# Q and K stored in runs of eight units per channel in an attention kernel on one core

## The chip, the cores and the metric

The kernel runs on one core of a Trainium2 chip. The metric is the device time of one execution in microseconds (us).

## The reference

The input is x of shape (8, 512, 256). After a layer norm, x is projected to Q, K and V, each 1024 wide, in segments of 128 tokens. A segment's 128 x 1024 block is then read as 16 heads of 128 rows by 64 channels, without a transpose: head h takes the 8 tokens 8h to 8h+7, and each token gives 16 rows of 64. Per head and segment:

```python
scores  = q @ k.T * scale                       # masked above the diagonal
att_dot = softmax(scores) @ v
sq, sk  = elu(q) + 1, elu(k) + 1
att_mem = (sq @ M) / (sq @ Z.T)
M, Z    = M + sk.T @ v, Z + sk.sum(rows)        # carried to the next segment
att     = gate * att_mem + (1 - gate) * att_dot
out     = att.reshape(128, 1024) @ Wo
```

A layer norm and a residual follow. Then comes a second block: three cycles of a small net of four layers that scales a "twist" of the row, and again a layer norm and a residual.

## The kernel before

Two sequences are worked on together as a pair, so a step is one pair and one of its 4 segments: 16 steps (`NT`), of which the first 12 run in a loop with four steps in its body. A step has 32 units (`UNITS`), a unit being one head of one of the two sequences. The units are handled in 4 groups g of 8 (`GU`), and in a group as 4 pairs (`GP`), because two units of 64 channels fill the 128 rows of the matmul array.

The order of the work is written out by hand, one function `step` for each engine, with semaphores between them:

- `project(i)`, L1109, TensorE: 12 fp16 matmuls make one half (32 channels) of Q (i = 0, 1), K (i = 2, 3) or V (i = 4, 5) of the *next* step in `x_bank`, a PSUM tile of 2 x 512 columns. Only one such tile exists, so `project(i + 1)` waits until half i has been taken out.
- `take_x(i)`, L814, VectorE: one instruction that transposes 32 x 32 blocks takes half i out of `x_bank` and stores it in `q_pos`, `k_pos` or `v_pos`. These hold in each partition one row of all 32 units, unit after unit, so a channel's 32 values are 64 words apart (68 for V).
- `turn(g)`, L1126, TensorE: transposes the four pairs of group g of Q and of K into a bank of `t_bank`. Each reads 128 consecutive words (two units side by side) as the weights of a matmul against the identity. Function `take_q` on ScalarE (L548 to L555) and VectorE (L823 to L828) turns them into fp16 parts for `scores(g)` (L1138, L1143).
- `exp_k(g)` (ScalarE, L564, L567) and `elu_k(g)` (GpSimd, L402, L405) make `sk`, which is elu(k) + 1 and has the layout of `k_pos`. `remember(g)`, L1187, TensorE, reads 128 consecutive words of `sk` as weights against two units of V, and VectorE adds the result to the memory `M` (L863). It isn't run in the last segment of a pair, so 12 of the 16 steps have it.
- `maxima` (L835), `probs` (L574), `turn_probs` (L1154), `read_out` (L1167, L1172), `divide` (L842, L845) and `gated` (L418 to L422) are the softmax, its product with V, the read from memory, and the gate. `to_rows` (L911, two instructions of VectorE) brings the attention back to token rows; `turn_att` (L1199) and `project_out` (L1214) multiply it with Wo.

`t_bank` has two banks that all the turning jobs share in a fixed order (`STEP_JOBS`). In particular `remember(0)` has two jobs, and the second (U0b) needs the bank that the next row tile (job N) leaves when VectorE's `split` (L775) has run; VectorE's order puts `split` right behind `take_x(3)`:

```python
                    y_norm(bp, s)
                    if not last:
                        take_x(bp, s, 3)
                    if ahead:
                        split(t_job(bp, s, "N"), s % 2, bp * NSEG + (s + 3))
                    maxima(bp, s, 2)
                    remember(bp, s, 0, last)
```

Of the kernel before, what the change touches and what calls it, by code (L numbers as in the profile page):

```python
# [5 lines left out]
ALU = mybir.AluOpType  # L6
ACT = mybir.ActivationFunctionType
# [17 lines left out]
GROUPS = 4  # L25
GU = UNITS // GROUPS
GP = GU // 2
DV1 = DK + 1
VS = DK + 4
EPS = 1e-5  # L30
# [34 lines left out]
def infini_block_kernel(nc, x, Wq, Wk, Wv, Wo, betas, memory0, z0, cw1, cb1, cw2, cb2, cw3, cb3,  # L65
                        cw4, cb4, gw1, gb1, gw2, gb2, gw3, gb3, adaptive_range, out):
    ctx = ExitStack()
    with ctx:
# [97 lines left out]
        assert top[0] <= gate_off, (top[0], gate_off)  # L166
        top[0] = attn_top

        def xt_cols(t, cols=2 * P):

            return bass.ds((t + 1) * 2 * P, cols)
# [119 lines left out]
        with nc.Block() as block:  # L291

            @block.sync
            def _(sp):
# [7 lines left out]
                sp.dma_start(Wo_sb, Wo.rearrange("(j p) n -> p j n", p=P)).then_inc(c_in, 16)  # L302
                for par in range(2):
                    sp.dma_start(M0[64 * par:64 * par + 64, :, 0:DK],
                                  memory0[0].rearrange("(j r) d e -> r d j e", r=2)[par]).then_inc(c_in, 16)
                    sp.dma_start(M0[64 * par:64 * par + 64, :, DK:DV1],
                                  z0[0].rearrange("(j r) a d -> r d j a", r=2)[par]).then_inc(c_in, 16)
# [58 lines left out]
            def _(pool):  # L366
# [30 lines left out]
                def elu_k(bp, s, g):  # L397

                    n = 4 * s + g
                    dst = sk[:, g * GU * DK:(g + 1) * GU * DK]  # L400
                    pool.wait_ge(ek_done, bp * 16 + n + 1)
                    pool.tensor_tensor(dst, dst, k_pos[s % 2][:, g * GU * DK:(g + 1) * GU * DK],  # L402
                                       ALU.add).then_inc(sk_part, 1)
                    pool.wait_ge(sk_part, bp * 16 + n + 1)
                    pool.tensor_tensor(dst, dst, ek, ALU.add).then_inc(sk_done, 1)  # L405

                def gated(bp, s, g, half):

                    n = 8 * s + 2 * g + half
                    mem, dot = (AB[half][:, m, :, :] for m in (1, 0))  # L410
                    u = GU * g + 4 * half
                    gt = gate[:, (u % H) * DK:(u % H + 4) * DK].rearrange("p (u e) -> p u e", u=4)
                    if n == 0:
                        pool.wait_ge(g_in, 16)
                    if g == 0 and half == 0:
                        pool.wait_ge(nat_done, bp * 8 + 2 * (s + 1))
                    pool.wait_ge(pm_free, bp * 32 + n + 2)
                    pool.tensor_tensor(mem, mem, dot, ALU.subtract).then_inc(mix, 1)  # L418
                    pool.wait_ge(mix, bp * 64 + 2 * n + 1)
                    pool.tensor_tensor(mem, mem, gt, ALU.mult).then_inc(mix, 1)  # L420
                    pool.wait_ge(mix, bp * 64 + 2 * n + 2)
                    pool.tensor_tensor(att[:, u * DK:(u + 4) * DK].rearrange("p (u e) -> p u e", u=4),  # L422
                                       mem, dot, ALU.add).then_inc(att_done, 1)

                def y_dev(bp, s):
# [84 lines left out]
            def _(act):  # L510
# [46 lines left out]

                def exp_k(bp, s, g):
                    n = 4 * s + g
                    cols = slice(g * GU * DK, (g + 1) * GU * DK)  # L560
# [6 lines left out]
                    act.activation(ek, sk[:, cols], ACT.Exp, scale=-1.0).then_inc(ek_done, 1)  # L567

                def probs(bp, s, g):
                    G = 4 * s + g  # L570
# [175 lines left out]
            def _(dve):  # L746
# [55 lines left out]
                def take_x(bp, s, i, first=False):  # L802


                    n = 6 if not first else 0
                    par = 0 if first else (s + 1) % 2
                    dve.wait_ge(x_full, bp * 24 + 6 * s + n + i + 1)
                    if not first and i == 2:

                        dve.wait_ge(sk_done, bp * 16 + (4 * s + 1))  # L810
                    dst = (q_pos, k_pos, v_pos)[i // 2][par].rearrange("p (u e) -> p e u", u=UNITS)
                    d0 = 32 * (i % 2)
                    bank = first_banks[i] if first else x_bank
                    dve.transpose(dst[:, d0:d0 + 32, :],  # L814
                                  bank.rearrange("p w (d c) -> p d w c", c=C)).then_inc(x_free, 1)

                def take_q(bp, s, g):
# [257 lines left out]
            def _(pe):  # L1075
# [81 lines left out]
                def read_out(bp, s, g, half):  # L1157

                    n = 8 * s + 2 * g + half
                    v = v_pos[s % 2].rearrange("p (u e) -> p u e", u=UNITS)  # L1160
# [4 lines left out]
                    for u in range(4):  # L1165
                        j, par = 2 * half + u // 2, u % 2
                        pe.matmul(pm_bank[:, 0, u * DV1:(u + 1) * DV1], PT[:, par, j, :],  # L1167
                                  v[:, GU * g + 2 * j + par, 0:DV1], start=True, stop=True)
# [7 lines left out]
                def remember(bp, s, g):  # L1176

                    if s == NSEG - 1:
                        return
                    v = v_pos[s % 2].rearrange("p (u e) -> p u e", u=UNITS)  # L1180
                    pe.wait_ge(sk_done, bp * 16 + (4 * s + g + 2))
                    for a in range(2):
                        b, n = t_job(bp, s, f"U{g}{'ab'[a]}")
                        pe.wait_ge(t_free[b], n)
                        for i in range(2):
                            u = GU * g + 4 * a + 2 * i
# [253 lines left out]
```

## Time and profile before

| what | value |
|---|---|
| time, median of 3 runs | 1279.06 us (1278.69 to 1281.06) |
| the profiled execution's own time | 1277.61 us |
| its span | 1275.8 us |
| TensorE matmul busy | 1084.4 us (85%) |
| TensorE weight load busy | 755.4 us (59%) |
| VectorE busy | 855.4 us (67%) |
| ScalarE busy | 611.2 us (48%) |
| GpSimd busy | 584.1 us (46%) |
| mean granted TensorE clock | 0.941 of full speed |

The attention part takes about the first 1060 us, the second block the rest. A weight load runs beside an earlier matmul, so its busy time is a row of its own (PEld) and not added to that of the matmuls (PE). A matmul with fp32 operands stands in the trace as two weight loads and two matmuls; an fp32 transpose stands as one of each.

### The profile page before, as it was taken

To read this page: it belongs to the slowest core of one execution; us is meant where nothing else is said; L and a number is where in the kernel's file an instruction comes from. 1 tells how busy PE (TensorE), PEld (TensorE's weight loads), DVE (VectorE), ACT (ScalarE), POOL (GpSimd) and SP (SyncE) were. 2 spreads that over 40 slices of the span, in tenths; PEclk is the share of its full clock that TensorE was granted. 3 is DMA by queue.
4 is the path that set the end of the run, shared out by engine and by line. 5 is a ranking of instruction groups with operands and counts; after the bars stand their busy time and mean duration, and the time that the engine had idled before them with its cause. 6 is when DMAs were issued, how large, how long until landed. Compare 5 with 4: busy or idle time off the path is not lost.

```text
span 1275.8 us, 20673 instructions
## 1 busy us (share of the span) xinstructions
PE 1084.4 (85%) x7172; PEld 755.4 (59%) x7172; DVE 855.4 (67%) x1492; ACT 611.2 (48%) x1291; POOL 584.1 (46%) x715
## 2 busy tenths in 40 slices
PE   3798989897888899878889888989888888999971
PEld 1475767664767676646666666676767675433331
DVE  4868686866686868656877687768686752434365
ACT  4354444444353535434545454535353553566662
POOL 2145454554454545444545454545454552322266
PEclk9999998988999989989999999999999988999995
DMA  5000000000000000000000000000000010300014
GB/s 161 20 10 9 10 9 10 10 11 9 10 9 9 9 10 10 10 11 2 17 10 9 9 10 9 10 10 9 9 2 9 1 28 1 140 0 0 1 33 99
DMA packets 14842, 24.02 MB, mean 19 GB/s; under 512 B 5264, under 2 KB 7056, under 8 KB 14224
## 3 DMA queue, kind: packets, MB, share of 16 engines
q1 hardware_dynamic: 14736, 22.63, 5.8%
q8 instruction: 63, 1.03, 0.3%
q14 instruction: 43, 0.35, 0.1%
HBM read 13.97 MB, written 8.65 MB: 18 GB/s over the span
## 4 chain that ended last, share of the span: by engine, by line
PE 49%; DVE 29%; issue 11%; ACT 7%; POOL 2%; DMA 1%; SPq 0%; DVEq 0%; POOLq 0%; ACTq 0%
PE ps L1109 12%; PE ps L1214 9%; DVE arena L814 7%; PE ps L1327 6%; PE ps L1167 5%; DVE arena L911 3%; PE ps L1340 3%; ACT arena L574 3%; PE ps L1172 3%; PE ps L1154 3%; DVE arena L758 2%; DVE arena L845 2%; DVE arena L824 2%; PE ps L1199 2%; DVE arena L828 2%
## 5 line engine op out<-in xcount | busy, mean ns | idle before, releaser
L1109 PE MATMUL ps<-arena 128*128 128x512 f16 x1152 | 274.0, 390 | 6.0 <-DVE arena L790 4.2
L574 ACT ACTIVATE arena<-ps,arena 128x128 f32<-128x128 f32 x512 | 139.3, 384 | 223.3 <-DVE arena L835 223.1
L814 DVE STREAM_TRANSPOSE arena<-ps 128x1024 f32<-128x1024 f32 x96 | 190.2, 1983 | 43.8 <-PE ps L1109 43.8
L1109 PEld LDWEIGHTS ps<-arena 128*128 128x128 f16 x1152 | 113.8, 100 | 131.8 <-issue 18.7
L418 POOL TENSOR_TENSOR arena<-arena 128x256 f32<-128x256 f32 x128 | 93.0, 727 | 161.7 <-DVE arena L845 161.7
L1167 PEld LDWEIGHTS ps<-arena 128*128 128x128 f32 x1024 | 134.8, 200 | 25.6 <-issue 17.3
L1167 PE MATMUL ps<-arena 128*128 128x65 f32 x1024 | 137.5, 280 | 13.2 <-DVE arena L845 11.8
L402 POOL TENSOR_TENSOR arena<-arena 128x512 f32<-128x512 f32 x64 | 81.3, 1270 | 125.5 <-ACT arena L567 125.5
L1214 PE MATMUL ps<-arena 128*128 128x256 f32 x544 | 122.0, 382 | 0.3 <-ACT arena L586 0.3
L388 POOL TENSOR_TENSOR arena<-arena 128x2 f32<-128x2 f32 x50 | 9.8, 196 | 238.8 <-DVE arena L754 238.8
L1214 PEld LDWEIGHTS ps<-arena 128*128 128x128 f32 x544 | 102.0, 190 | 16.1 <-ACT arena L586 1.4
L750 DVE BATCH_NORM_STATS2 arena<-arena 128x6 f32<-128x256 f32 x100 | 36.7, 409 | 111.0 <-ACT arena L592 97.4
L1154 PE MATMUL ps<-arena 128*128 128x128 f32 x512 | 82.7, 299 | 30.6 <-ACT arena L574 30.2
L1187 PE MATMUL ps<-arena 128*128 128x130 f32 x384 | 66.9, 312 | 41.4 <-DVE arena L775 24.1
L420 POOL TENSOR_TENSOR arena<-arena 128x256 f32<-128x256 f32 x128 | 93.1, 727 | 10.0
L422 POOL TENSOR_TENSOR arena<-arena 128x256 f32<-128x256 f32 x128 | 93.0, 727 | 10.0
L845 DVE TENSOR_TENSOR arena<-ps,arena 128x512 f32<-128x512 f32 x128 | 88.5, 691 | 13.1 <-DVE arena L842 0.8
L580 ACT ACTIVATE arena<-ps 128x1024 f32<-128x1024 f32 x64 | 65.7, 1026 | 64.4 <-PE ps L1154 64.4
L758 DVE TENSOR_SCALAR arena<-arena 128x256 f32<-128x256 f32 x100 | 68.7, 727 | 36.7 <-POOL arena L390 36.7
L1154 PEld LDWEIGHTS ps<-arena 128*128 128x128 f32 x512 | 62.5, 152 | 48.9 <-ACT arena L574 48.1
L835 DVE TENSOR_REDUCE arena<-ps 128x4 f32<-128x512 f32 x128 | 81.7, 678 | 12.5 <-PE ps L1143 12.1
L1327 PE MATMUL ps<-arena 128*128 128x512 f32 (+1 forms) x192 | 89.3, 609 | 0.8 <-ACT arena L687 0.8
(109 smaller groups left out, 1873.5 us busy)
## 6 DMA issues: line engine op xcount, KB each, us to landing
x_rows<-arena SPq DMA_DIRECT2D x17, 256.0 KB, 2.0
arena<-in_L_attn_x_dram SPq DMA_DIRECT2D x64, 64.0 KB
arena<-x_rows SPq DMA_DIRECT2D x4, 1024.0 KB, 8.0
out_dram<-arena SPq DMA_DIRECT2D x32, 128.0 KB, 2.9
arena<-in_L_attn_Wq_dram SPq DMA_DIRECT2D x1, 1024.0 KB, 12.2
arena<-in_L_attn_Wk_dram SPq DMA_DIRECT2D x1, 1024.0 KB, 14.4
arena<-in_L_attn_Wv_dram SPq DMA_DIRECT2D x1, 1024.0 KB, 17.4
arena<-in_L_attn_Wo_dram SPq DMA_DIRECT2D x1, 1024.0 KB, 13.0
```

Of the source, the lines that this page charges most:

```text
L418: pool.tensor_tensor(mem, mem, dot, ALU.subtract).then_inc(mix, 1)
L420: pool.tensor_tensor(mem, mem, gt, ALU.mult).then_inc(mix, 1)
L422: pool.tensor_tensor(att[:, u * DK:(u + 4) * DK].rearrange("p (u e) -> p u e", u=4), mem, dot, ALU.add).then_inc(att_done, 1)
L574: last = act.activation(Pr[:, par, j, :], s_bank[:, par, j * P:(j + 1) * P], ACT.Exp, bias=negm[:, par, j:j + 1])
L758: last = dve.tensor_scalar(dst[:, w * D:(w + 1) * D], src[:, w * D:(w + 1) * D], mv[:, w, 0:1], rs[:, w:w + 1], ALU.subtract, ALU.mult)
L814: dve.transpose(dst[:, d0:d0 + 32, :], bank.rearrange("p w (d c) -> p d w c", c=C)).then_inc(x_free, 1)
L845: dve.tensor_tensor(AB[half], rd[:, :, :, 0:DK], rr.rearrange("p m (u a) -> p m u a", a=1).to_broadcast([P, 2, 4, DK]), ALU.mult).then_inc ...
L1109: last = pe.matmul(bank[:, w, :], xc[:, lx, k, w * P:(w + 1) * P], W16[lw][:, k, i, :], start=(n == 0), stop=(n == 5))
L1154: last = pe.transpose(s_bank[:, par, j * P:(j + 1) * P], Pr[:, par, j, :], identf)
L1167: pe.matmul(pm_bank[:, 0, u * DV1:(u + 1) * DV1], PT[:, par, j, :], v[:, GU * g + 2 * j + par, 0:DV1], start=True, stop=True)
L1214: last = pe.matmul(t_bank[b][:, w * D:(w + 1) * D], attT[:, w, j, :], Wo_sb[:, j, :], start=(j == 0), stop=(j == 7))
L1327: done = pe.matmul(l1_bank[2 * j + c], w1[:, k, c * P:(c + 1) * P], XT[:, k, bass.ds((bb * 4 + (2 * j + 1)) * 2 * P, NB)], start=(k == 0), ...
```

## The change

A unit u is now written as u = 16 y + 8 r + h, with y the sequence of the pair, r = 0 or 1, and h = 0 to 7. `q_pos`, `k_pos` and `sk` are laid out as (y r, channel, h): for each channel, eight units (h) stand side by side. A pair is now made of units h and h + 8, no longer of two neighbours, and its 128 weights (r, channel) are read with a step of 8 words. `take_x` writes Q and K in runs of 8 words. V keeps its layout with a channel's units 68 words apart; its two units of a pair are now 8 units apart. The memory is loaded with the new pairing, the gate and the attention output are addressed accordingly, and `exp_k` and `elu_k` now work on runs of 4 words (the four pairs of a group). `ek` is written and read without gaps.

No instruction is added, removed or moved on any engine or queue, and none has another number of elements; what differs is how operands are addressed. The diff's core:

```diff
+HP = H // 2
+        def heads(a):
+            return a.rearrange("p (y z h) -> p y h z", y=2, h=HP)
+        def group(a, g):
+            return a.rearrange("p (y z h) -> p y z h", y=2, h=HP)[:, g // 2, :, GP * (g % 2):GP * (g % 2) + GP]
...
-                                  memory0[0].rearrange("(j r) d e -> r d j e", r=2)[par]).then_inc(c_in, 16)
+                                  memory0[0].rearrange("(r j) d e -> r d j e", r=2)[par]).then_inc(c_in, 16)
...
 # elu_k, GpSimd
-                    dst = sk[:, g * GU * DK:(g + 1) * GU * DK]
+                    dst, k = group(sk, g), group(k_pos[s % 2], g)
...
 # gated, GpSimd
-                    pool.tensor_tensor(att[:, u * DK:(u + 4) * DK].rearrange("p (u e) -> p u e", u=4),
+                    pool.tensor_tensor(att.rearrange("p (y r h e) -> p y h r e", y=2, r=2, h=HP)[:, g // 2, h:h + 2],
...
 # exp_k, ScalarE
-                    act.activation(sk[:, cols], k_pos[s % 2][:, cols], ACT.Relu, scale=-1.0).then_inc(rk_done, 1)
+                    act.activation(part, group(k_pos[s % 2], g), ACT.Relu, scale=-1.0).then_inc(rk_done, 1)
...
 # take_x, VectorE
-                    dst = (q_pos, k_pos, v_pos)[i // 2][par].rearrange("p (u e) -> p e u", u=UNITS)
+                    dst = (q_pos, k_pos, v_pos)[i // 2][par].rearrange(
+                        "p (u e) -> p e u" if i >= 4 else "p (v e h) -> p e v h", **(
+                            dict(u=UNITS) if i >= 4 else dict(v=UNITS // HP, h=HP)))
...
 # turn, TensorE
-                            u = GU * g + 2 * j
                             last = pe.transpose(t_bank[b][:, j * P:(j + 1) * P],
-                                                src[par][:, u * DK:(u + 2) * DK], identf)
+                                                heads(src[par])[:, g // 2, GP * (g % 2) + j], identf)
...
 # remember, TensorE
                             last = pe.matmul(t_bank[b][:, i * 2 * DV1:(i + 1) * 2 * DV1],
-                                             sk[:, u * DK:(u + 2) * DK], v[:, u:u + 2, 0:DV1],
+                                             heads(sk)[:, g // 2, h], v[:, h, :, 0:DV1],
                                              start=True, stop=True)
```

## Rows read from the trace of the kernel before

**Rows 1.** The page: busy time of each engine, and the chain's shares by engine.

```profile
PE 1084.4 (85%) x7172; PEld 755.4 (59%) x7172; DVE 855.4 (67%) x1492; ACT 611.2 (48%) x1291; POOL 584.1 (46%) x715
...
PE 49%; DVE 29%; issue 11%; ACT 7%; POOL 2%; DMA 1%; SPq 0%; DVEq 0%; POOLq 0%; ACTq 0%
```

**Rows 2.** Timeline of PE, us 434 to 500: start, us, engine, line, count, [idle before].

```profile
440.56 1.04 PE L1126 MATMUL ps<-arena 128*128 128x128 f32 x8
...
447.04 0.59 PE L1138 MATMUL ps<-arena 128*128 128x512 bf16 x2 [1.52 <-DVE arena L824]
...
449.79 1.08 PE L1167 MATMUL ps<-arena 128*128 128x65 f32 x8 [0.35 <-DVE arena L845]
...
464.36 0.60 PE L1126 MATMUL ps<-arena 128*128 128x128 f32 x4
...
472.02 1.24 PE L1187 MATMUL ps<-arena 128*128 128x130 f32 x4 [2.19 <-DVE arena L775]
...
475.62 1.94 PE L1187 MATMUL ps<-arena 128*128 128x130 f32 x8
...
487.36 0.71 PE L1187 MATMUL ps<-arena 128*128 128x130 f32 x4 [1.13 <-DVE arena L893]
...
496.07 1.06 PE L1187 MATMUL ps<-arena 128*128 128x130 f32 x8
497.44 1.08 PE L1167 MATMUL ps<-arena 128*128 128x65 f32 x8 [0.31 <-DVE arena L845]
```

**Rows 3.** Timeline of DVE, the same stretch: takes 0, 1 and 3 and their neighbours.

```profile
438.82 1.98 DVE L814 STREAM_TRANSPOSE arena<-ps 128x1024 f32<-128x1024 f32 x1 [0.42 <-PE ps L1109]
440.83 4.37 DVE L911 STREAM_TRANSPOSE arena<-arena 128x1024 f32<-128x1024 f32 x2
...
446.87 1.93 DVE L814 STREAM_TRANSPOSE arena<-ps 128x1024 f32<-128x1024 f32 x1
...
453.99 1.98 DVE L814 STREAM_TRANSPOSE arena<-ps 128x1024 f32<-128x1024 f32 x1 [1.66 <-PE ps L1109]
...
469.53 1.91 DVE L814 STREAM_TRANSPOSE arena<-ps 128x1024 f32<-128x1024 f32 x1
471.31 0.66 DVE L775 TENSOR_TENSOR arena<-ps,arena 128x512 f16<-128x512 f32 x1
```

**Rows 4.** Groups by line and form: count, busy us, mean ns, idle before.

```profile
L814 DVE STREAM_TRANSPOSE arena<-ps 128x1024 f32<-128x1024 f32 x96 | 190.2, 1983 | 43.8 <-PE ps L1109 43.8
...
L911 DVE STREAM_TRANSPOSE arena<-arena 128x1024 f32<-128x1024 f32 x34 | 74.2, 2243 | 2.1 <-POOL arena L422 1.6
...
L835 DVE TENSOR_REDUCE arena<-ps 128x4 f32<-128x512 f32 x128 | 81.7, 678 | 12.5 <-PE ps L1143 12.1
...
L1015 DVE BATCH_NORM_STATS2 arena<-ps 128x6 f32<-128x256 f32 x32 | 12.0, 415 | 0.0
```

**Rows 5.** The same view: ScalarE on 1024 elements, without and with a stepped read.

```profile
L580 ACT ACTIVATE arena<-ps 128x1024 f32<-128x1024 f32 x64 | 65.7, 1026 | 64.4 <-PE ps L1154 64.4
...
L515 ACT ACTIVATE arena<-arena 128x1024 f16<-128x1024 f32 x6 | 11.3, 1946 | 5.0 <-DMA arena<-in_L_attn_Wq_dram 5.0
```

**Rows 6.** The same view: the weight loads that the change touches, and GpSimd's part of `sk`.

```profile
L1126 PEld LDWEIGHTS ps<-arena 128*128 128x128 f32 x512 | 62.3, 148 | 12.6 <-DVE arena L863 6.0 <-issue 4.1
L1187 PEld LDWEIGHTS ps<-arena 128*128 128x128 f32 x384 | 55.4, 212 | 48.5 <-DVE arena L775 26.2 <-DVE arena L893 17.6 <-issue 2.2
...
L402 POOL TENSOR_TENSOR arena<-arena 128x512 f32<-128x512 f32 x64 | 81.3, 1270 | 125.5 <-ACT arena L567 125.5
```

**Rows 7.** Timeline of PEld: one `turn` and one `remember` of eight loads.

```profile
431.82 0.97 PEld L1187 LDWEIGHTS ps<-arena 128*128 128x128 f32 x8
...
440.45 0.91 PEld L1126 LDWEIGHTS ps<-arena 128*128 128x128 f32 x8
```

**Rows 8.** Windows: length, busy PE, PEld, DVE, ACT, POOL, granted clock, DMA share.

```profile
472.00:479.00 7.00, 6.98 (x33) 6.98 (x34) 4.95 (x14) 2.18 (x8) 1.17 (x2) 0.51 0.10 36
...
607.00:614.00 7.00, 7.00 (x51) 5.24 (x50) 5.56 (x18) 5.77 (x14) 2.47 (x5) 1.00 0.01 3
```

More of the change, by code:

```diff
@@ L304, in _ @@
                     sp.dma_start(M0[64 * par:64 * par + 64, :, 0:DK],
-                                  memory0[0].rearrange("(j r) d e -> r d j e", r=2)[par]).then_inc(c_in, 16)
+                                  memory0[0].rearrange("(r j) d e -> r d j e", r=2)[par]).then_inc(c_in, 16)
                     sp.dma_start(M0[64 * par:64 * par + 64, :, DK:DV1],
-                                  z0[0].rearrange("(j r) a d -> r d j a", r=2)[par]).then_inc(c_in, 16)
+                                  z0[0].rearrange("(r j) a d -> r d j a", r=2)[par]).then_inc(c_in, 16)
                 for dst, src in blocks(xrow[2], x_rows, 0, 2):
@@ L399, in elu_k @@
                     n = 4 * s + g
-                    dst = sk[:, g * GU * DK:(g + 1) * GU * DK]
+                    dst, k = group(sk, g), group(k_pos[s % 2], g)
                     pool.wait_ge(ek_done, bp * 16 + n + 1)
-                    pool.tensor_tensor(dst, dst, k_pos[s % 2][:, g * GU * DK:(g + 1) * GU * DK],
-                                       ALU.add).then_inc(sk_part, 1)
+                    pool.tensor_tensor(dst, dst, k, ALU.add).then_inc(sk_part, 1)
                     pool.wait_ge(sk_part, bp * 16 + n + 1)
-                    pool.tensor_tensor(dst, dst, ek, ALU.add).then_inc(sk_done, 1)
+                    pool.tensor_tensor(dst, dst, ek.rearrange("p (z h) -> p z h", h=GP),
+                                       ALU.add).then_inc(sk_done, 1)
                 def gated(bp, s, g, half):
                     n = 8 * s + 2 * g + half
-                    mem, dot = (AB[half][:, m, :, :] for m in (1, 0))
-                    u = GU * g + 4 * half
-                    gt = gate[:, (u % H) * DK:(u % H + 4) * DK].rearrange("p (u e) -> p u e", u=4)
+                    mem, dot = (AB[half][:, m, :, :].rearrange("p (h r) e -> p h r e", r=2) for m in (1, 0))
+                    h = GP * (g % 2) + 2 * half
+                    gt = gate.rearrange("p (r h e) -> p h r e", r=2, h=HP)[:, h:h + 2]
                     if n == 0:
@@ L559, in exp_k @@
                     n = 4 * s + g
-                    cols = slice(g * GU * DK, (g + 1) * GU * DK)
+                    part = group(sk, g)
                     if g == 0:
@@ L563, in exp_k @@
                     memory_stands(act, bp, s, g)
-                    act.activation(sk[:, cols], k_pos[s % 2][:, cols], ACT.Relu, scale=-1.0).then_inc(rk_done, 1)
+                    act.activation(part, group(k_pos[s % 2], g), ACT.Relu, scale=-1.0).then_inc(rk_done, 1)
                     act.wait_ge(rk_done, bp * 16 + n + 1)
                     act.wait_ge(sk_done, bp * 16 + (n + 1))
-                    act.activation(ek, sk[:, cols], ACT.Exp, scale=-1.0).then_inc(ek_done, 1)
+                    act.activation(ek.rearrange("p (z h) -> p z h", h=GP), part, ACT.Exp, scale=-1.0).then_inc(ek_done, 1)
                 def probs(bp, s, g):
@@ L810, in take_x @@
                         dve.wait_ge(sk_done, bp * 16 + (4 * s + 1))
-                    dst = (q_pos, k_pos, v_pos)[i // 2][par].rearrange("p (u e) -> p e u", u=UNITS)
+                    dst = (q_pos, k_pos, v_pos)[i // 2][par].rearrange(
+                        "p (u e) -> p e u" if i >= 4 else "p (v e h) -> p e v h", **(
+                            dict(u=UNITS) if i >= 4 else dict(v=UNITS // HP, h=HP)))
                     d0 = 32 * (i % 2)
                     bank = first_banks[i] if first else x_bank
-                    dve.transpose(dst[:, d0:d0 + 32, :],
+                    dve.transpose(dst[:, d0:d0 + 32],
                                   bank.rearrange("p w (d c) -> p d w c", c=C)).then_inc(x_free, 1)
@@ L1159, in read_out @@
                     n = 8 * s + 2 * g + half
-                    v = v_pos[s % 2].rearrange("p (u e) -> p u e", u=UNITS)
+                    v = v_pos[s % 2].rearrange("p (y r h e) -> p y h r e", y=2, r=2, h=HP)[:, g // 2]
                     pe.wait_ge(p_done, bp * 16 + 4 * s + g + 2)
@@ L1167, in read_out @@
                         pe.matmul(pm_bank[:, 0, u * DV1:(u + 1) * DV1], PT[:, par, j, :],
-                                  v[:, GU * g + 2 * j + par, 0:DV1], start=True, stop=True)
+                                  v[:, GP * (g % 2) + j, par, 0:DV1], start=True, stop=True)
                     memory_stands(pe, bp, s, g)
@@ L1179, in remember @@
                         return
-                    v = v_pos[s % 2].rearrange("p (u e) -> p u e", u=UNITS)
+                    v = v_pos[s % 2].rearrange("p (y r h e) -> p y h r e", y=2, r=2, h=HP)[:, g // 2]
                     pe.wait_ge(sk_done, bp * 16 + (4 * s + g + 2))
@@ L1185, in remember @@
                         for i in range(2):
-                            u = GU * g + 4 * a + 2 * i
+                            h = GP * (g % 2) + 2 * a + i
                             last = pe.matmul(t_bank[b][:, i * 2 * DV1:(i + 1) * 2 * DV1],
-                                             sk[:, u * DK:(u + 2) * DK], v[:, u:u + 2, 0:DV1],
+                                             heads(sk)[:, g // 2, h], v[:, h, :, 0:DV1],
                                              start=True, stop=True)
```

## The prediction

> **What bounds the kernel now.** I read the page's engine line first, then the chain, then the timelines of one step, then the groups by form. The page has TensorE's matmuls busy 85% of the span, VectorE 67%, but the chain that ended last gives TensorE only 49% and VectorE 29% [rows 1]. So neither engine alone sets the end: work passes between them. The timeline of one step shows where. The step from 434.7 to 498.9 us lasts 64.1 us, and TensorE stands still in it at a few places, nearly all ended by VectorE: 1.52 us before `scores(1)`, 0.35 us before `read_out(0, 1)`, 2.19 us before the second job of `remember(0)`, 1.13 us before that of `remember(2)`, 0.31 us before `read_out(3, 1)` [rows 2]. Between these TensorE runs without a gap. A saving on VectorE counts where it shortens such a wait; a loss on TensorE counts where it isn't swallowed by one.
>
> **The takes of Q and K.** `take_x` needs 1.98 us for 1024 elements per partition [rows 4]. The same engine, reading PSUM without a step, needs 0.415 us for 256 elements and 0.678 us for 512 [rows 4], which is 1.03 ns per further element, so 1024 would cost 0.678 + 512 x 1.03 ns = 1.21 us. The transposes of `to_rows`, stepped on both sides, need 2.24 us [rows 4]: a second stepped side adds 0.26 us, so steps do cost a transpose time. I take 1.22 us for a take that writes runs of 8 words, a saving of 0.76 us. The bounds are 0 (if the transposing itself is the slow part) and 0.8 us. The Trainium skill, Vector Engine (DVE) Microarchitecture Reference, section Measured stream behaviour on trn2, says that a port runs at full rate when its words come in aligned runs of two or more, and gives 1.71 ns per element for a hopping destination; the trace's 1.98 us over 1024 elements is near that. Four of six takes per step change (64 of the 96), some 49 us of VectorE's time. V's don't.
>
> What this buys, in the step shown, if nothing else changed:
> - Take 0 starts at 438.82 and `to_rows` follows it without a gap [rows 3]. All of it, `take_q(1)` behind it and so `scores(1)` come 0.76 us earlier; TensorE's 1.52 us wait has room for it.
> - Take 1 (446.87) stands before `divide(0, 0)`, which ends the 0.35 us wait [rows 2, 3]. TensorE gains that too: 1.1 us in all.
> - Take 2 waits 1.66 us for TensorE [rows 3] and ends no wait of TensorE. It gives nothing.
> - Take 3 (469.53) is followed by `split` at 471.31, which ends the 2.19 us wait [rows 2, 3]: a further 0.76 us.
>
> That is 1.9 us per step, 30 us over 16 steps, and 3 us at the start, where the first takes stand alone.
>
> **The weight loads.** `turn` has 32 loads per step and `remember` 32 in the 12 steps that have it: 512 and 384 [rows 6]. They follow one another closely: eight in 0.91 us and eight in 0.97 us [rows 7], that is one per 0.11 to 0.12 us, or 0.9 ns for each of the 128 words. As the eight matmuls of the turn take 1.04 us [rows 2], the load is what paces them, and a slower load would lengthen TensorE's own work. The trace has no stepped weight load, so I bound it. Low end: no cost, if TensorE fetches ahead. High end: the worst rate of any stepped access in the trace, 2243 / 1024 = 2.19 ns per word [rows 4], that is 280 ns per load, 0.17 us more than now. Between lies the cleanest pair of rows: ScalarE does 1024 elements in 1.026 us without a step and in 1.946 us with a stepped read [rows 5], 0.90 ns more per word. VectorE's take and ScalarE's stepped copy come to almost the same 1.9 ns per element although the engines differ, which speaks for a limit on the memory's side that a weight load would meet as well. I take 128 x 0.90 = 0.115 us more per load, 0.11 in the sums.
>
> The Trainium skill speaks on both sides. Advanced Engine Details and Errata, section SBUF Cachelines, says that accesses that each hit another 16-byte line pay a penalty, and a step of 8 words is 32 bytes; that is against this change, and it goes with my price. TensorE: Matmul & The Clock Gate, section LDWEIGHTS (loading the stationary operand), gives a load's time by its columns alone, P / 1.2 ns; by it the step is free, which is the first rival. The Trainium skill's Vector Engine (DVE) Microarchitecture Reference, in the section named above, has 2.50 ns for a step of 24 words, worse than for long ones; by an estimate from that figure a load would cost 0.21 us more, which is beyond rival 2. No row here shows any of the three for TensorE.
>
> **What the slower loads cost on the path.** Again in the step shown, in order, with 0.11 us per load:
> - `turn(1)`: 8 loads, 0.9 us. TensorE had 1.52 us of waiting behind it, of which 0.76 us is now gone; it just fits. TensorE stays 1.1 us ahead.
> - `turn(2)`, Q and K: 8 loads, 0.9 us. TensorE is then 0.3 us ahead. But the wait for `split` hangs on VectorE, which followed `project_out` and is some 0.75 us ahead, and with take 3 1.5 us. The first job of `remember(0)` is slower too, in that same wait. The wait shrinks from 2.19 to about 1 us and ends 1.5 us earlier.
> - the second job of `remember(0)`, `remember(1)`, `turn(3)`: 20 loads, 2.2 us without a wait to hide in, so TensorE is 0.8 us behind. VectorE, which left this row of work after `remember(1)`, is even. So the wait for L893 (1.13 us) swallows the 0.8 and nearly all of the 0.45 us of `remember(2)`'s first job.
> - its second job: 0.45 us, swallowed by the wait for ScalarE's exponentials. `turn(0)`: 0.9 us, and `remember(3)`: 0.9 us, less the 0.31 us wait [rows 2]: 1.4 to 1.5 us behind at the step's end.
>
> Sum with `remember`: +1.4 us. In the four steps without it only the turns count and the saving outweighs them: about -0.5 us.
>
> **The clock.** Behind the 2.19 us wait the granted clock is at 0.51 in one step, that is the lower of its two levels (1.2 GHz), and at 1.00 in another [rows 8]; eight matmuls of `remember` take 1.94 us at the lower and 1.06 us at the full level [rows 2]. About half of the steps fall there. With the wait cut to half I expect fewer falls, worth 0.4 us per step; the bounds are 0 and 0.9.
>
> **The rest.** ScalarE's and GpSimd's operands in runs of 4 words: I cost them at nothing. GpSimd waits 125.5 us in total before L402 [rows 6] and is 46% busy, ScalarE 48% [rows 1]. Were each of the 128 instructions of `elu_k` (1.27 us) to double, that would be 10 us per step on an engine with 34 us of rest, and only the residual add, queued behind `elu_k(2)`, would come late, by 2.5 us, with more than that before VectorE's statistics need it. The loads of the initial memory move the same bytes: nothing. `read_out` and `remember` read V in the same runs of 65 words: nothing.
>
> **Sum.** 12 x (1.4 - 0.4) + 4 x (-0.5 - 0.4) - 3 = 5.4 us. The swallowing above is exact to a few tenths per step, and take 1 and the falls of the clock may not give all that I credit; I round up to +10 us. The profiled execution took 1277.6 us, 1.5 us below the median of the runs: 1288 us, and the median with it within that 1.5 us. Its own range: -10 to +25 us, 1268 to 1303.
>
> **The rivals.**
> 1. *The step is free for weight loads.* For it: TensorE's reads may be buffered, and nothing in the trace shows the opposite. Against: two engines pay alike. Then the 1.9 us per step stay whole and the clock adds 0.4: 16 x 2.3 + 3 = 40 us less, **1238 us** (1225 to 1250).
> 2. *The loads become the bound.* At 0.17 us more per load `turn(1)` uses its whole wait, `turn(2)` eats the lead at `split`, and the wait for L893 no longer swallows `turn(3)` and `remember(1)`. The point from which it decides is some 0.12 us per load: up to there the waits hold most of it, beyond it nearly every load counts. Worked through in the same way, a step with `remember` ends 4.6 us behind and one without 2 us: 55 + 8, less 6 for the clock, **1335 us** (1305 to 1355).
> 3. *The takes get no shorter*, as the transposing is the slow part. Against it: `to_rows` reacts to a second stepped side. With the loads at +0.11 us, a step loses the 1.9 us too and ends about 3 us behind: **1330 us**.
>
> **How the numbers follow.** Forecast 0.34, rival 1 0.34, rival 2 0.25, rival 3 0.07. The forecast is the middle case and keeps a small edge, as the rows give its price directly. A measurement of this kernel can tell about 0.2%, 2.6 us. Rival 1 is faster throughout; of the forecast's 0.34, 0.08 lies below -2.6 us, 0.06 within, 0.20 above; rivals 2 and 3 are slower. Faster 0.42, same 0.06, slower 0.52. The range must reach into rivals 1 and 2: 1232 to 1348 leaves out about 0.2.
>
> **What would show it.** In the changed kernel the 64 takes of Q and K should last 1.2 us beside V's 32 at 1.98. The weight loads of `turn` and `remember` should follow one another at 0.22 us; at 0.11 rival 1 holds, at 0.28 or more rival 2. The wait for `split` should be 1 us or less, and the clock should fall less often behind it. GpSimd's two instructions of `elu_k` should stay near 1.27 us; if they go above 3 us, my cover for them is gone. I am wrong if the loads keep their pace, or if the takes don't change.

## The result and the profile after

| | before | changed |
|---|---|---|
| median, 20 runs each | 1279.04 us | 1269.98 us |
| lowest to highest | 1276.79 to 1281.11 us | 1264.41 to 1280.85 us |
| span of the profiled execution | 1275.8 us | 1262.6 us |

The ratio is 0.9933, with a 95% interval of 0.9918 to 0.9948: 9 us faster, where 10 us slower was forecast. The changed kernel's runs scatter more than those before, and their time goes with the granted clock: 0.948 of full speed in the profiled execution of 1264.41 us, 0.928 and 0.929 in those of 1277.19 and 1280.85 us. So the one profiled execution, at the fast end, is read for mechanisms and not for the size.

The page of the changed kernel, engines and chain, as in [rows 1]:

```profile
PE 1111.2 (88%) x7172; PEld 796.9 (63%) x7172; DVE 819.3 (65%) x1492; ACT 610.9 (48%) x1291; POOL 584.7 (46%) x715
...
PE 55%; DVE 25%; issue 9%; ACT 5%; POOL 2%; DMA 1%; SPq 0%; DVEq 0%; POOLq 0%; ACTq 0%
```

VectorE lost 36 us of work, TensorE gained 27 us of matmul time and 41 us of load time, and the chain moved towards TensorE. The groups say which instructions changed (lines are 9 to 11 higher than before: L825 is the take, L1136 the turn, L1197 `remember`, L411 `elu_k`):

```profile
L825 DVE STREAM_TRANSPOSE arena<-ps 128x1024 f32<-128x1024 f32 x96 | 145.2, 1514 | 40.3 <-PE ps L1120 40.3
...
L1197 PEld LDWEIGHTS ps<-arena 128*128 128x128 f32 x384 | 97.0, 332 | 28.4 <-DVE arena L784 13.8 <-DVE arena L904 11.5 <-issue 0.6
...
L411 POOL TENSOR_TENSOR arena<-arena 128x512 f32<-128x512 f32 x64 | 81.4, 1272 | 118.1 <-ACT arena L576 118.1
...
L1136 PEld LDWEIGHTS ps<-arena 128*128 128x128 f32 x512 | 71.0, 195 | 10.2 <-DVE arena L874 6.3 <-issue 2.2
```

Against [rows 4] and [rows 6]: the takes fell from 190.2 to 145.2 us in sum, GpSimd stayed at 1.27 us. A load of `remember` lasts 332 ns instead of 212, one of the turn 195 instead of 148. But a duration isn't a pace; loads overlap. The pace is in the timeline of TensorE, us 425 to 500, with the same columns as [rows 2]; L1148 is `scores(1)`, L784 `split` (L775 before), L904 (L893) VectorE's sums that the second job of `remember(2)` waits for, and L874 (L863) its part of `remember`:

```profile
435.80 1.04 PE L1136 MATMUL ps<-arena 128*128 128x128 f32 x8
...
441.63 0.59 PE L1148 MATMUL ps<-arena 128*128 128x512 bf16 x2 [0.86 <-DVE arena L835]
...
465.43 1.22 PE L1197 MATMUL ps<-arena 128*128 128x130 f32 x4 [1.07 <-DVE arena L784]
...
479.69 1.23 PE L1197 MATMUL ps<-arena 128*128 128x130 f32 x4 [0.84 <-DVE arena L904]
...
483.87 1.34 PE L1136 MATMUL ps<-arena 128*128 128x128 f32 x8 [0.39 <-DVE arena L874]
...
488.97 2.07 PE L1197 MATMUL ps<-arena 128*128 128x130 f32 x8
```

Eight matmuls of a turn still take 1.04 us: stepped loads don't slow them. Eight of `remember` take 2.07 us instead of 1.06 [rows 2], 0.13 us more for each. The wait for `split` fell from 2.19 to 1.07 us, the one before `scores(1)` from 1.52 to 0.86, the one for L893 from 1.13 to 0.84, and the 0.31 and 0.35 us waits are gone. A new one of 0.39 us stands before `turn(0)`. VectorE's own rows show the shortened takes 0, 1 and 3 in the same step and the take of V (476.15) unchanged:

```profile
434.08 1.25 DVE L825 STREAM_TRANSPOSE arena<-ps 128x1024 f32<-128x1024 f32 x1 [0.44 <-PE ps L1120]
435.36 4.43 DVE L922 STREAM_TRANSPOSE arena<-arena 128x1024 f32<-128x1024 f32 x2
...
441.41 1.28 DVE L825 STREAM_TRANSPOSE arena<-ps 128x1024 f32<-128x1024 f32 x1
...
463.56 1.24 DVE L825 STREAM_TRANSPOSE arena<-ps 128x1024 f32<-128x1024 f32 x1
...
476.15 2.05 DVE L825 STREAM_TRANSPOSE arena<-ps 128x1024 f32<-128x1024 f32 x1
```

The step shown runs at the full clock. At the lower level the loss is nearly gone. These are the eight matmuls of `remember(1)` in two other steps, before and after; the granted clock meanwhile was 0.50 (411.5 to 413.3) and 0.54 (405.7 to 407.6):

```profile
411.48 1.94 PE L1187 MATMUL ps<-arena 128*128 128x130 f32 x8
...
405.66 2.00 PE L1197 MATMUL ps<-arena 128*128 128x130 f32 x8
```

Eight stepped loads take about 2 us at either level (2.07 and 2.00), while eight without a step take 1.15 at the full one (at 608.30 us, the same place) and 1.94 at the lower. So the stepped loads' pace didn't follow the clock, and the step's cost of 0.9 us at the full level is 0.06 at the lower.

So two theories were put to the chip. A: an ordinary fp32 matmul pays for a stepped load and an fp32 transpose doesn't. B: all stepped loads are slow, and waits in the kernel hid it in the turns. Beside them stood the question how large the gain and the loss are by themselves.

### The profile page after: what moved, and what is told of

The parts are those of the page before. It is cut to its first block, busy times and chain, and to the rows that moved or that the text cites. A ratio compares the mean times of both kernels' runs of the same rounds, so it can differ in the third digit from the quotient of the medians.

```text
span 1262.6 us, 20673 instructions
## 1 busy us (share of the span) xinstructions
PE 1111.2 (88%) x7172; PEld 796.9 (63%) x7172; DVE 819.3 (65%) x1492; ACT 610.9 (48%) x1291; POOL 584.7 (46%) x715
## 4 chain that ended last, share of the span: by engine, by line
PE 55%; DVE 25%; issue 9%; ACT 5%; POOL 2%; DMA 1%; SPq 0%; DVEq 0%; POOLq 0%; ACTq 0%
PE ps L1120 10%; PE ps L1224 10%; PE ps L1337 6%; PE ps L1197 6%; PE ps L1177 5%; DVE arena L825 5%; DVE arena L922 4%; PE ps L1182 3%; PE ps L1350 3%; PE ps L1209 3%; PE ps L1164 2%; DVE arena L767 2%; DVE arena L835 2%; PE ps L1153 2%; DVE arena L834 2%
## 5 line engine op out<-in xcount | busy, mean ns | idle before, releaser
L1120 PE MATMUL ps<-arena 128*128 128x512 f16 x1152 | 268.3, 384 | 5.1 <-DVE arena L799 4.2
L825 DVE STREAM_TRANSPOSE arena<-ps 128x1024 f32<-128x1024 f32 x96 | 145.2, 1514 | 40.3 <-PE ps L1120 40.3
L1177 PEld LDWEIGHTS ps<-arena 128*128 128x128 f32 x1024 | 135.2, 201 | 16.2 <-issue 7.9
L411 POOL TENSOR_TENSOR arena<-arena 128x512 f32<-128x512 f32 x64 | 81.4, 1272 | 118.1 <-ACT arena L576 118.1
L1197 PE MATMUL ps<-arena 128*128 128x130 f32 x384 | 107.9, 416 | 21.3 <-DVE arena L784 11.7
L1197 PEld LDWEIGHTS ps<-arena 128*128 128x128 f32 x384 | 97.0, 332 | 28.4 <-DVE arena L784 13.8
L1224 PEld LDWEIGHTS ps<-arena 128*128 128x128 f32 x544 | 102.0, 190 | 16.1 <-ACT arena L595 1.4
L1182 PE MATMUL ps<-arena 128*128 128x130 f32 x512 | 92.0, 305 | 0.0
```

The costliest lines, as they stand in the source:

```text
L825: dve.transpose(dst[:, d0:d0 + 32], bank.rearrange("p w (d c) -> p d w c", c=C)).then_inc(x_free, 1)
L1120: last = pe.matmul(bank[:, w, :], xc[:, lx, k, w * P:(w + 1) * P], W16[lw][:, k, i, :], start=(n == 0), stop=(n == 5))
L1182: last = pe.matmul(pm_bank[:, 1, a * 2 * DV1:(a + 1) * 2 * DV1], sqT[g % 2][:, j, :], M[:, GP * g + j, :, :], start=True, stop=True)
L1224: last = pe.matmul(t_bank[b][:, w * D:(w + 1) * D], attT[:, w, j, :], Wo_sb[:, j, :], start=(j == 0), stop=(j == 7))
```

## The experiments

Ratios are to the kernel before, measured together with each run, with 95% intervals. Of the edits the main lines are shown; `...` marks what is left out.

### m1_steps: single instructions back to back

The kernel leaves out the whole computation and issues rows of 20 to 40 equal instructions (3 each on the other engines). Only the step of one operand differs between rows:

```python
for i in range(20): pe.matmul(ps[:, i % 4, 0:130], cols(a, STEP), a[:, 0:130], start=True, stop=True)
for i in range(40): pe.transpose(ps[:, i % 4, 0:128], cols(a, STEP), idt)
for i in range(40): pe.matmul(ps[:, i % 4, 0:128], cols(h, STEP), h[:, 0:128], start=True, stop=True)   # fp16
```

> The whole computation is left out; the kernel measures single instructions back to back and writes x to the output. Theory A (an ordinary fp32 matmul pays for a stepped weight load, an fp32 transpose doesn't): fp32 matmuls of 130 columns with weights stepped by 8 words follow one another at 0.24 to 0.26 us per load against 0.11 without a step, transposes at 0.11 with and without, fp16 matmuls unknown. Rival B (every stepped weight load is slower, and in the changed kernel the turns hid it): transposes in a long row go above 0.11 us with a step of 8 words. A step of 2 words should be free if pairs of words in one 16-byte line are what counts, and as slow as 8 if any step is slow. VectorE's transposes: 1.9 us with single words, 1.25 us from runs of 2 words on if pairs suffice, from runs of 4 on if whole lines are needed. ScalarE on 512 elements: 0.62 us without a step, about 1.1 us reading single words 8 apart, 0.62 us in runs of 4. GpSimd on 512: 1.27 us, unchanged in runs of 4, 1.3 to 1.9 us with one input stepped.

The timeline of TensorE (start, us, line, count). L103 to L109 are the fp32 matmul with weights stepped by 1, 2, 3, 4, 8, 16 and 64 words; L110 and L112 to L115 the transpose at 1, 4, 8, 16 and 64; L116, L119 and L121 the fp16 matmul at 1, 8 and 64; L122 and L123 are the fp32 matmul with 256 moving columns, weights stepped by 1 and 8; L124 has the *moving* operand stepped by 8 words, L125 by 1:

```profile
24.46 4.63 PE L103 MATMUL ps<-a 128*128 128x130 f32 x40
28.92 4.87 PE L104 MATMUL ps<-a 128*128 128x130 f32 x40
33.63 7.10 PE L105 MATMUL ps<-a 128*128 128x130 f32 x40
40.57 9.49 PE L106 MATMUL ps<-a 128*128 128x130 f32 x40
49.90 9.76 PE L107 MATMUL ps<-a 128*128 128x130 f32 x40
59.50 8.90 PE L108 MATMUL ps<-a 128*128 128x130 f32 x40
68.23 8.96 PE L109 MATMUL ps<-a 128*128 128x130 f32 x40
77.03 4.53 PE L110 MATMUL ps<-idt,a 128*128 128x128 f32 x40
...
86.19 5.01 PE L112 MATMUL ps<-idt,a 128*128 128x128 f32 x40
91.04 4.63 PE L113 MATMUL ps<-idt,a 128*128 128x128 f32 x40
95.51 4.70 PE L114 MATMUL ps<-idt,a 128*128 128x128 f32 x40
100.04 6.03 PE L115 MATMUL ps<-idt,a 128*128 128x128 f32 x40
105.91 2.40 PE L116 MATMUL ps<-hh 128*128 128x128 f16 x40
...
112.61 2.62 PE L119 MATMUL ps<-hh 128*128 128x128 f16 x40
...
117.54 3.78 PE L121 MATMUL ps<-hh 128*128 128x128 f16 x40
121.16 8.85 PE L122 MATMUL ps<-a 128*128 128x256 f32 x40
129.85 9.76 PE L123 MATMUL ps<-a 128*128 128x256 f32 x40
139.44 9.49 PE L124 MATMUL ps<-a 128*128 128x128 f32 x40
148.75 4.65 PE L125 MATMUL ps<-a 128*128 128x128 f32 x40
```

Divided by 40, an fp32 matmul goes from 0.12 us to 0.12 at a step of 2 words, 0.18 at 3 and 0.24 at 4 and 8. A transpose stays at 0.11 to 0.13 up to 16 words, in a long row without waits; at 64 words it needs 0.15. So B falls, and A holds for the pace. An fp16 matmul goes from 0.06 to 0.07 at 8 elements and to 0.09 at 64. A moving fp32 operand pays like a weight.

The steps of 1, 2, 3, 4 and 8 words let the 128 words of a load fall into 32, 64, 96, 128 and 128 different stretches of 16 bytes. From 2 words on the time of the ordinary fp32 matmul follows this count at 1.9 ns per stretch: 0.12, 0.18, 0.24, 0.24. That is a fit and no mechanism: steps of 16 and 64 words need a little less (0.22), and an fp16 load with a step of 8 elements, also one stretch for each, stays at 0.07.

Two things hide a slow load. With 256 moving columns a matmul without a step takes 0.22 us, and with a step of 8 words 0.24, the same as with 130 columns: there the slow load costs 0.02 us instead of 0.13. And a transpose goes at 0.11 us without a step, so a load of up to that length can't show in its pace. Whether its load got slower below that, no row separates. Its recorded duration did grow, from 143 ns without a step to 193 at 8 words. Why it stays at half of an ordinary fp32 load is open.

On VectorE (L135 writes single words 64 apart, L136 runs of 2 words, L138 runs of 8), ScalarE (L146: 512 words read singly, 8 apart; the read without a step took 0.63 us):

```profile
L135 DVE STREAM_TRANSPOSE o<-ps 128x1024 f32<-128x1024 f32 x3 | 5.7, 1894 | 137.0 <-PE ps L127 136.9
...
L136 DVE STREAM_TRANSPOSE o<-ps 128x1024 f32<-128x1024 f32 x3 | 3.8, 1251 | 0.1
...
L138 DVE STREAM_TRANSPOSE o<-ps 128x1024 f32<-128x1024 f32 x3 | 3.7, 1249 | 0.1
...
L146 ACT ACTIVATE o<-a 128x512 f32<-128x512 f32 x3 | 3.5, 1150 | 0.1
```

Runs of 2 words are enough for VectorE; runs of 8 bring nothing more. The Trainium skill, Vector Engine (DVE) Microarchitecture Reference, section Measured stream behaviour on trn2, says just this of VectorE's ports, and the row at 1251 ns agrees.

ScalarE and GpSimd weren't measured with both sides in runs of 4. With one side at single words they took 1.13 to 1.15 and 1.52 us for 512 elements; in the changed kernel, with runs of 4, `exp_k`'s two instructions last 0.62 and 0.63 us and `elu_k`'s 1.27, as before. GpSimd's very first add lasted 5.50 us instead of 1.27, beside a cast of 4.43 us on VectorE; e9 comes back to this.

### e3_takes_only: the gain alone

```diff
 # kernel before
-                    dst = (q_pos, k_pos, v_pos)[i // 2][par].rearrange("p (u e) -> p e u", u=UNITS)
+                    dst = (q_pos, k_pos, v_pos)[i // 2][par].rearrange(
+                        "p (u e) -> p e u" if i >= 4 else "p (v e h) -> p e v h", **(
+                            dict(u=UNITS) if i >= 4 else dict(v=4, h=8)))
...
```

Q and K are still read as if unit lay after unit, so this kernel doesn't compute the attention; its instructions are the same.

> The kernel before, with Q and K taken in runs of 8 words and read as before without a step, so the output isn't the reference's. Theory A: the whole gain of the shorter takes shows, 1.9 us per step and a little of the clock: 30 to 45 us faster than before, 1235 to 1250. Rival C (the takes are mostly hidden and bring little; remember's loads cost little): 8 to 20 us faster.

Measured: 1246.32 us, ratio 0.9738 [0.972, 0.9756], 33.8 us less. The prediction's sum for the takes is 16 x 1.9 + 3 = 33 us, and 40 with the clock, its first rival. The measured gain is that of the takes alone.

### e1_remember_step: one loss alone

```diff
 # kernel before: sk alone in the new layout
...
+                    part = sk.rearrange("p (y z h) -> p y z h", y=2, h=8)[:, g // 2, :, GP * (g % 2):GP * (g % 2) + GP]
...
-                                             sk[:, u * DK:(u + 2) * DK], v[:, u:u + 2, 0:DV1],
+                                             sk.rearrange("p (y z h) -> p y h z", y=2, h=8)[:, g // 2, GP * (g % 2) + 2 * a + i], v[:, u:u + 2, 0:DV1],
```

> The kernel before, with sk alone in the new layout (written and read in runs of 4 words, its weight loads stepped by 8 words); its K isn't regrouped, so the memory part isn't the reference's. Theory A: the 384 loads of remember go from 0.11 to 0.25 us each, 2.2 us in a row of 16 whose ends lie on the path, and some of the rest: 20 to 45 us slower than before. Rival B (the loads of remember are swallowed by waits and the turns are what costs): within 8 us of before.

Measured: 1303.79 us, ratio 1.0193 [1.0172, 1.0213], 23.6 us more. 384 loads at 0.126 us more would be 48 us of TensorE, and about half of that doesn't reach the time: part goes into waits (the wait for `split` fell from 24.1 to 18.8 us in total, the one for L893 from 15.3 to 7.5), and at the lower clock a stepped load costs almost nothing. This run also wrote and read `sk` in runs of 4 words, with GpSimd's instructions at 1.27 us and ScalarE's at 0.62 and 0.63 as before.

### e2_turn_step: the other loss alone

```diff
 # kernel before
-                                                src[par][:, u * DK:(u + 2) * DK], identf)
+                                                src[par].rearrange("p (y z h) -> p y h z", y=2, h=8)[:, u // 16, u % 16 // 2], identf)
```

> The kernel before, with the 512 loads of the turns of Q and K stepped by 8 words and nothing else; they read other words than they should, so the output isn't the reference's. Theory A: loads last 0.19 us instead of 0.14 but follow one another at 0.11 as before: within 3 us of before. Rival B: 5 to 30 us slower.

Measured: 1282.45 us, ratio 1.0024 [1.0011, 1.0038], 2.3 us more by the medians and 3 by the ratio. The loads last 195 ns as in the changed kernel, at the old pace. A's bound of 3 us is just met. Where the 2 to 3 us come from stays open: a turn that starts behind a wait takes 1.34 us instead of 1.28, and 4 such places per step would make 3 us, but that wasn't isolated; the granted clock was also a little lower (0.935 against 0.938, medians of the runs).

The three parts together are -33.8 + 23.6 + 2.3 = -7.9 us, and the whole change measured -9.1. The parts nearly add up.

### e4_sk_pairs: the loss undone

In the changed kernel `sk` is stored pair after pair again. ScalarE and GpSimd bridge the two layouts.

```diff
 # elu_k
-                    dst, k = group(sk, g), group(k_pos[s % 2], g)
+                    dst = sk[:, g * GU * DK:(g + 1) * GU * DK].rearrange("p (h z) -> p z h", h=GP)
+                    k = group(k_pos[s % 2], g)
...
 # exp_k
-                    part = group(sk, g)
+                    part = sk[:, g * GU * DK:(g + 1) * GU * DK]
...
 # remember
-                                             heads(sk)[:, g // 2, h], v[:, h, :, 0:DV1],
+                                             sk[:, (8 * (g // 2) + h) * P:(8 * (g // 2) + h + 1) * P], v[:, h, :, 0:DV1],
```

> The changed kernel with one part undone: sk is stored pair after pair, so remember's weight loads have no step again, while Q, K and the turns stay as changed. ScalarE's first pass of exp_k then pays about 1.15 us instead of 0.62 and GpSimd's first add 1.53 instead of 1.27. Theory (the takes gain about 33 us, the turns' stepped loads cost 2 to 3, remember's stepped loads 25): 1247 to 1252, about 20 us below the changed kernel. Rival (the loss in the changed kernel lies in the runs of 4 words or in the new pairing, not in the loads): 1262 or more.

Measured: 1259.13 us, ratio 0.9836 [0.9806, 0.9866]. Faster than the changed kernel, but 7 us above the top of what the theory expected. Its trace shows where: the wait for `split` is back at 2.33 us although take 3 is short.

```profile
464.96 0.71 PE L1199 MATMUL ps<-arena 128*128 128x130 f32 x4 [2.33 <-DVE arena L786]
```

VectorE's `y_norm` in front of that take (L769, two instructions) runs while GpSimd does `elu_k(2)`:

```profile
460.56 2.61 DVE L769 TENSOR_SCALAR arena<-arena 128x256 f32<-128x256 f32 x2
463.10 1.24 DVE L827 STREAM_TRANSPOSE arena<-ps 128x1024 f32<-128x1024 f32 x1
464.26 0.65 DVE L786 TENSOR_TENSOR arena<-ps,arena 128x512 f16<-128x512 f32 x1
```

```profile
460.15 1.53 POOL L412 TENSOR_TENSOR arena<-arena 128x512 f32<-128x512 f32 x1 [1.88 <-ACT arena L578]
461.76 1.26 POOL L415 TENSOR_TENSOR arena<-arena 128x512 f32<-128x512 f32 x1
```

L769 ends at 463.17, right behind the end of L415 at 463.02. The two instructions take 1.86 us at this place in the changed kernel, and 2.61 us here, where GpSimd's first add is 0.26 us longer and starts 0.41 us before them instead of 0.91, so that more of its two adds lies beside them.

### e9_sk_pairs_swap: the overlap taken away

```diff
 # GpSimd's step, on e4_sk_pairs
-                    elu_k(bp, s, 2)
                     residual(bp, s)
+                    elu_k(bp, s, 2)
```

> The kernel with sk stored pair after pair, with elu_k(2) moved behind the residual add in GpSimd's order. In that kernel VectorE's two instructions of y_norm, in front of take 3, last 2.61 us while GpSimd's elu_k(2) runs, against 1.86 in the changed kernel and 0.73 where GpSimd is idle. If that overlap is what kept it at 1259 instead of 1247 to 1252: y_norm at 0.73 to 0.9 us, take 3 and split 1.7 us earlier, 1238 to 1248. Rival (the gap comes from ScalarE's longer pass of exp_k): no more than 4 us from 1259.

Measured: 1231.32 us, ratio 0.9625 [0.9609, 0.9641]: 27 to 28 us less than without the swap, more than the 11 to 21 expected. `y_norm` takes 0.73 us, and the wait for `split` is 0.45 us:

```profile
445.11 0.73 DVE L769 TENSOR_SCALAR arena<-arena 128x256 f32<-128x256 f32 x2
```

```profile
447.63 0.71 PE L1199 MATMUL ps<-arena 128*128 128x130 f32 x4 [0.45 <-DVE arena L786]
```

Both fell by 1.88 us, which over 16 steps is 30 us, so nearly the whole overlap lay on the path. In the 11 steps where the waits' view lists the wait for `split`, it fell from 25.6 to 4.7 us in total.

The Trainium skill, SBUF — State Buffer, section Who interferes with whom, says that VectorE and GpSimd share a pair of ports; VectorE takes it in its two-port mode, which tensor_scalar and casts can enter, and whoever issues first holds it for a whole instruction. The rows agree: VectorE's two instructions of tensor_scalar end 0.15 us behind GpSimd's second add, in e4 (463.17 and 463.02) and before (469.61 and 469.46). In m1_steps it is the other way round: the cast on VectorE ends at 17.37 us, and GpSimd's add, issued 0.05 us after it, at 18.49. The ports themselves stand in no trace.

The overlap is in the kernel before as well, at 1.83 us for the two:

```profile
467.78 1.83 DVE L758 TENSOR_SCALAR arena<-arena 128x256 f32<-128x256 f32 x2
```

The walk through the step took that duration as given. A second `y_norm` per step, beside the gate's products on GpSimd, still lasts 1.61 us in e9.

### e6, e7, e8, e10: runs of two

The table of steps suggests a layout without the loss: pair units two apart and store runs of 2. A group is then contiguous for ScalarE and GpSimd as well.

```diff
 # e6, on the kernel before
+                        "p (u e) -> p e u" if i >= 4 else "p (v e h) -> p e v h", **(
+                            dict(u=UNITS) if i >= 4 else dict(v=UNITS // 2, h=2)))
... (the memory's load, the gate and V's readers follow the new pairing)
+                                                src[par].rearrange("p (q z h) -> p q h z", q=8, h=2)[:, 2 * g + j // 2, j % 2], identf)
...
+                                             sk.rearrange("p (q z h) -> p q h z", q=8, h=2)[:, 2 * g + a, i], v[:, 2 * g + a, i, :, 0:DV1],
 # e7, on e6: nat in runs of 8, its turns with a step of 8 words; Wo's rows are loaded in the new order
+                        dve.transpose(nat.rearrange("p (v e j) -> p e v j", v=4, j=8)[:, 32 * e:32 * e + 32],
...
+                                            nat.rearrange("p (w z j) -> p w j z", w=2, j=8)[:, i // 2, j],
 # e8, on e7: V in runs of 2
+                    dst = (q_pos, k_pos, v_pos)[i // 2][par].rearrange("p (v e h) -> p e v h", v=UNITS // 2, h=2)
 # e10, on e8: elu_k(2) behind the residual add, as in e9
```

> Units two apart paired and Q, K and sk stored in runs of 2 units per channel: weight loads with a step of 2 words, and a group of units is one contiguous stretch again for ScalarE and GpSimd. If a pair of words is what the memory fetches, the takes need 1.25 us and remember's loads 0.12 us: 1244 to 1250, below both kernels. If any step costs remember its pace: about 1270 as in the changed kernel.

> As the kernel with runs of 2, and nat in runs of 8 words with its transposes reading weights stepped by 8 words. to_rows then writes in runs but still reads single words: its two instructions go from 2.24 to about 1.95 us, 0.5 to 0.6 us per step in front of take_q(1), part of which ends TensorE's wait before scores(1). Where that wait is already short: 0 to 8 us below runs of 2. The turns show 0.11 us per load.

> As the one before, with V in runs of 2 as well, so that TensorE's moving operand has a step of 2 words. All 96 takes at 1.25 us. Take 4 stands before the sums that end the wait of remember(2)'s second job, take 5 is behind the step's last reads. If a moving operand of pairs keeps its pace: 8 to 15 us below the one before, about 1230. If a stepped moving operand slows down even in pairs: slower than the one before by 10 us or more.

> The kernel with all in runs of 2, with the same move. The wait for split falls by up to 1.1 us per step, so 1208 to 1218 if all of it is on the path; 1220 or more if elu_k(2), now later, makes remember(2) or the second take of K wait.

| kernel | median | ratio to before, interval |
|---|---|---|
| e6_runs_of_2 | 1247.54 us | 0.9752 [0.9728, 0.9777] |
| e7_runs_of_2_nat | 1233.96 us | 0.9646 [0.963, 0.9662] |
| e8_all_runs_of_2 | 1224.42 us | 0.9568 [0.9554, 0.9581] |
| e10_all_swap | 1207.29 us | 0.9435 [0.9415, 0.9456] |

e6 lands where the takes alone did, so with a step of 2 words the loads cost nothing that these intervals could show. That it beats the changed kernel by 22 us with equally short takes also fits a loss that lay in `remember`'s step of 8 words. e7 brings 14 us where 0 to 8 were expected. Its `to_rows` instructions fell from 2.26 to 1.96 us each, 0.6 us per step or 10 us; the rest is hardly more than the intervals of the two (about 3 and 2 us). e8 comes out as expected (8 to 15 us), e10 1 us better than its range: it is the fastest kernel of this study, 72 us below the one before. In its profile all takes are short and `y_norm`'s group (L762) has a mean of 548 ns against 727 for all its uses before:

```profile
L762 DVE TENSOR_SCALAR arena<-arena 128x256 f32<-128x256 f32 x100 | 50.7, 548 | 38.1 <-POOL arena L394 38.1
...
L818 DVE STREAM_TRANSPOSE arena<-ps 128x1024 f32<-128x1024 f32 x96 | 119.5, 1245 | 40.7 <-PE ps L1113 40.7
```

## Why the prediction was wrong

- **The takes** were right: 1.22 us forecast, 1.25 measured (1.24 to 1.28 in the step shown), and V's stayed at 2.0. What they bring, 1.9 us per step and 30 to 40 us in all, was right too: 33.8 us in e3.
- **The turns' loads** were the step that failed. I priced 512 loads at 0.11 us more each; they cost 0 at their pace, and 2 to 3 us in the whole kernel (e2). In the sum they were what turned the sign: the same walk without them gives -8.6 instead of +5.4 us, as worked out below. I had taken one price for all stepped loads because ScalarE and VectorE agreed with each other. That argued from two engines to a third, and the two kinds of load already differed in the trace of before: 148 ns for a transpose's load and 212 ns for an ordinary one [rows 6], at nearly the same pace [rows 7]. I used the paces and passed over the durations. And "the load is what paces them" wasn't shown by the 1.04 us of a turn. The trace of before has fp32 matmuls with more and with fewer moving columns than 128:

```profile
444.02 1.00 PE L1167 MATMUL ps<-arena 128*128 128x65 f32 x8
...
455.57 7.17 PE L1214 MATMUL ps<-arena 128*128 128x256 f32 x32
```

  With 256 columns one takes 0.22 us, with 65 still about 0.12. So at 128 columns an ordinary load and the matmul's own pass are about equally long, and a transpose's load, shorter by its duration, may have had room.
- **The loads of `remember`** were about right: 0.115 us more each forecast, 0.13 measured in the kernel at the full clock and by itself. Of the 48 us that this makes, 24 reached the time (e1); the walk lets 31 through, 12 x (0.7 + 1.9). I had no term for the lower clock level, at which the step costs these loads almost nothing.
- **The walk through the step** held in its direction, and its closeness is partly luck. With the turns at nothing and `remember` at 0.126 us per load ((2.07 - 1.06) / 8) the same working gives, behind `split`: 1.5 us ahead, less 12 loads, even; 0.5 us swallowed at L904, 0.5 by the exponentials, and 1.0 less 0.3 at `remember(3)`, so +0.7 us in a step with `remember` and -1.9 in one without. 12 x (0.7 - 0.4) + 4 x (-1.9 - 0.4) - 3 = -8.6 us. The measured change is -9.1. This was worked out after the result, so it shows only that one price was enough to turn the sign. Taken apart, the walk gives 40 us for the takes where e3 measured 33.8, and 31 us for `remember` where e1 measured 23.6: two misses of 6 to 8 us that cancel.
- **The wait for `split`** at about 1 us: right, 1.07. **The clock**: the wait was to fall less often into the lower level. Behind it, 6 of 11 steps before run `remember(1)` at the lower level, 4 of 11 in the changed kernel's (fast) execution, and none in e9, where the wait is 0.45 us. What those 2 of 11 gave isn't separated, and e3's 33.8 us, against 33 for the takes without the clock, leave little for the 6 us that I had credited. **GpSimd and ScalarE in runs of 4**: at nothing, right: GpSimd 1272 ns, ScalarE 621 and 631.
- **The rivals.** Rival 1 (a step is free) was half true: free for transposes, not for ordinary fp32 matmuls. None of my cases had the two kinds apart; the result, 1270, lies between the forecast and rival 1, inside the range but on the other side of no change. Rival 2's sum leaves out the 3 us at the start that the others count: it comes to 1332 us.
- **Overlooked in the rows**: `y_norm` at 1.83 us for two instructions that last 0.73 us elsewhere. It stood right in front of take 3 on the path that I walked, and moving GpSimd's work away from it brought 17 us (e10 against e8) to 28 us (e9 against e4), more than V's takes (10 us, e8 against e7).

## What to carry to other kernels

Before a layout change puts a step into a weight load, ask which instruction it feeds: an fp32 transpose took a step of 8 words at full pace, an ordinary fp32 matmul of 130 columns took twice the time, one of 256 columns a tenth more, and a step of 2 words was nearly free for all that were tried. Store in runs of two words first; on VectorE they gave all that runs of 8 gave. And compare each instruction on the path with its own duration elsewhere in the trace: one that is 2.5 times longer at one place may be held up by another engine where no semaphore shows it.

## What the runs showed of the hardware that I had not expected

- fp32 weight loads by step, us per matmul and load: 0.12 at 1 and 2 words, 0.18 at 3, 0.24 at 4 and 8, 0.22 at 16 and 64, with 130 moving columns at the full clock. With 256 moving columns 0.22 without a step and 0.24 at 8. At the lower clock level a step of 8 words cost eight of them 0.06 us instead of 0.9. A moving fp32 operand stepped by 8 words: 0.24 against 0.12.
- The fp32 transpose: 0.11 to 0.13 up to a step of 16 words, 0.15 at 64. Its load's recorded duration grows (148 to 195 ns in the kernel) while its pace doesn't.
- fp16 loads with 128 columns follow one another at 0.06 us, with a step of 8 or 16 elements at 0.07.
- Two `y_norm` instructions of VectorE: 0.73 us alone, 1.83 to 2.61 us beside GpSimd's adds, with up to 28 us of the kernel's time behind it. A GpSimd add of 1.27 us: 5.50 us when it starts 0.05 us after a cast of 4.43 us on VectorE.
